# A macaron transformer kernel: the top-1 experts' bias-and-push product on four 32-row groups of TensorE, two tiles at a time, with three pairs of PSUM banks

## What is computed

```python
x = x + 0.5 * L0_ffn(layernorm(x))      # phase 0: F, 8 dense experts
x = x + L0_attn(layernorm(x))           # phase 1: R, RWKV mixing
x = x + 0.5 * L0_ffn(layernorm(x))      # phase 2: F
x = x + 0.5 * L1_ffn(layernorm(x))      # phase 3: E, top-1 of 8 experts
x = x + L1_attn(layernorm(x))           # phase 4: M, causal attention, 16 heads
x = x + 0.5 * L1_ffn(layernorm(x))      # phase 5: E

def L1_ffn(x):                          # D = 128, E = 8
    probs = softmax(einsum('bsd,ed->bse', x, router_w) + router_b)
    y_all = einsum('bsd,eod->bseo', x, expert_w) + expert_b
    return y_all[argmax(probs)] * max(probs)
```

## Time and profile before

| | us |
|---|---|
| median of 3 runs (1590.17 to 1595.67) | 1595.37 |
| profiled execution, whole | 1591.5 |
| its span in the trace | 1589.6 |
| PE busy in the span | 1541.5 (97%) |
| DVE busy in the span | 1260.2 (79%) |

### The profile page before, as it was taken

One profiled execution on the slowest core, in us unless ns is written; L12 is line 12 of the kernel. 1 busy time (PEld: TensorE's weight loads), 2 busy tenths in 40 slices (PEclk: granted clock), 3 DMA queues, 4 the chain that ended last, 5 costly groups with the idle time before them and its releaser, 6 DMA issues. The chain is left out here.

```text
span 1589.6 us, 43810 instructions
## 1 busy us (share of the span) xinstructions
PE 1541.5 (97%) x15808; PEld 922.1 (58%) x15808; DVE 1260.2 (79%) x2662; ACT 936.1 (59%) x1826; POOL 935.5 (59%) x806
## 2 busy tenths in 40 slices
PE   7999999999999899799999999999999999999999
PEld 4666666666666666566666666666654434444444
DVE  7976776777877788786777777768778899999877
ACT  6755555555656344365555555556553388888842
POOL 2865756757754399775766756657456334444453
PEclk9999999999999999999999999999999899999999
DMA  4300000000001242100000000000001121112011
GB/s 163 106 8 5 7 0 7 7 0 7 8 1 34 53 84 67 42 6 3 8 1 7 7 0 7 7 0 8 5 12 31 44 61 37 39 39 62 9 42 60
DMA packets 74315, 43.34 MB, mean 27 GB/s; under 512 B 53818, under 2 KB 70842, under 8 KB 74052
## 3 DMA queue, kind: packets, MB, share of 16 engines
q1 hardware_dynamic: 74180, 41.56, 10.9%
HBM read 10.47 MB, written 2.10 MB: 8 GB/s over the span
## 5 line engine op out<-in xcount | busy, mean ns | idle before, releaser
L618 POOL TENSOR_TENSOR scratch<-scratch 128x512 f16<-128x512 f32 x379 | 441.6, 1166 | 375.4 <-ACT scratch L826 375.2
L1395 DVE SCALAR_TENSOR_TENSOR scratch<-psum,scratch 128x512 f32<-128x512 f32 x512 | 352.4, 689 | 235.8 <-PE psum L1979 213.4
L821 ACT ACTIVATE scratch<-psum 128x512 f32<-128x512 f32 x512 | 305.2, 597 | 394.9 <-PE psum L1979 394.0
L2021 PE MATMUL psum<-ffn_down_hi,scratch 128*128 128x128 f16 x2048 | 369.3, 219 | 0.3
L2023 PE MATMUL psum<-ffn_down_hi,scratch 128*128 128x128 f16 x2048 | 369.2, 219 | 0.0
L2022 PE MATMUL psum<-ffn_down_lo,scratch 128*128 128x128 f16 x2048 | 369.2, 219 | 0.0
L826 ACT ACTIVATE scratch<-scratch 128x512 f16<-128x512 f32 x512 | 318.6, 622 | 12.0 <-DVE scratch L1395 11.7
L2021 PEld LDWEIGHTS psum<-ffn_down_hi,scratch 128*128 128x128 f16 x2048 | 200.3, 98 | 59.1 <-POOL scratch L618 0.7
L2022 PEld LDWEIGHTS psum<-ffn_down_lo,scratch 128*128 128x128 f16 x2048 | 200.4, 98 | 58.0
L2023 PEld LDWEIGHTS psum<-ffn_down_hi,scratch 128*128 128x128 f16 x2048 | 200.4, 98 | 0.0
L1977 PE MATMUL psum<-x_hi,ffn_gate_hi 128*128 (+1 forms) x512 | 194.5, 380 | 1.5 <-ACT scratch L821 1.5
(11 more groups left out here) (223 smaller groups left out, 2703.8 us busy)
## 6 DMA issues: line engine op xcount, KB each, us to landing
scratch<-scratch SPq DMA_DIRECT2D x96, 128.0 KB, 2.7
raw<-in_ffn_w_dram SPq DMA_DIRECT2D x8, 768.0 KB, 4.2
ffn_up_hi<-scratch SPq DMA_DIRECT2D x32, 128.0 KB, 2.8
x_tok<-in_x_dram SPq DMA_DIRECT2D x8, 256.0 KB, 7.2
out_dram<-x_tok SPq DMA_DIRECT2D x7, 256.0 KB, 2.2
raw<-in_lin_dram SPq DMA_DIRECT2D x1, 1092.0 KB
x_hi<-scratch SPq DMA_TRANSPOSE x46, 2.3
x_lo<-scratch SPq DMA_TRANSPOSE x46, 2.3
```

The source lines that it names most:

```text
L618: pool.tensor_tensor(h_lo[r], h32[r], h_hi[r], ALU.subtract).then_inc(s_plo, 1)
L821: act.activation(gate_act[k % 2], bank(k % 2), ACT.Silu, scale=W_DOWN).then_inc(s_s, 1)
L1395: dve.scalar_tensor_tensor(h32[k % HSLOTS], bank(5 + k % 2), W_DOWN, gate_act[k % 2], ALU.mult, ALU.mult).then_inc(s_h, 1)
L2021: pe.matmul(dst, h_hi[r][:, cols], hi, start=k % FC == 0 and n == 0, stop=False, skip_group_check=True)
```

## The change

The two matmuls of `bias_and_others` use only 10 rows of the array (8 pushes and 2 bias rows). Now their weights, and the rows that they meet, exist four times, on partitions 0, 32, 64 and 96. The bias's two halves of 512 columns stand beside each other on different partition groups (`e_bias`, loaded by 12 small DMAs from `bias_w` between the E phase's first and second `turn_x`). `e_not` has 128 columns for each tile (8 used in each of four groups of 32), so that `others` yields four copies of the rows. For two tiles together, four matmuls of 32 rows, each into a bank of its own, take the place of four with 128 rows. So in batches that have a next one, bias 0 moves behind products 1 and bias 2 behind products 3. In the last batch of a phase, and in the pieces woven into other phases, each tile's two matmuls are issued alone, also in 32-row form.

Tiles take the pairs of banks by `expert_banks`: three pairs in most of both phases, two at their borders. `products` waits for the pick of the last tile that had the same pair. `others` uses bank 6 in place of 4. `logits` adds the router's bias by one matmul of 32 columns for four tiles. PE's hardware loop over batches 2 to 5 is written out. A wait for the picks stands ahead of the attention's first projections.

```diff
-E_OUT = 2.0 ** 15
+E_OUT = 2.0 ** 14
+E_PUSH = 2.0 ** 16 - 2.0 ** 12
+E_GROUP = 32
...
-        e_not = carve(SUB * E, F16)
+        e_not = raw[:, 0:S // 2].bitcast(F16)
+        e_bias = raw[:, S // 2:S // 2 + BANK // 2].bitcast(F16)
...
+        def expert_banks(t):
+
+            if t < 2:
+                return t
+            if t < NS - 3:
+                return (2, 1, 0)[(t - 2) % 3]
+            if t < NS + SUB:
+                return t % 2
+            return (t - NS - SUB) % 3
+
+        def picked_before(t):
+
+            return 3 + max([s for s in range(t) if expert_banks(s) == expert_banks(t)], default=-1)
...
-            for b in range(3):
-                turn_x(3, b)
-            for b in range(3, NB):
+            turn_x(3, 0)
+            sp.wait_ge(s_erows, 3)
+            sp.wait_ge(s_blo, 2)
+            for i in range(4):
+                c = slice(i % 2 * BANK, (i % 2 + 1) * BANK)
+                row = i * E_GROUP
+                sp.dma_start(e_bias[row:row + E, :], bias_w[0:E, c]).then_inc(s_ebias, 16)
+                sp.dma_start(e_bias[row + E:row + E + 1, :], bias_w[32:33, c]).then_inc(s_ebias, 16)
+                sp.dma_start(e_bias[row + E + 1:row + E + 2, :], bias_w[64:65, c]).then_inc(s_ebias, 16)
+            for b in range(1, NB):
                 turn_x(3, b)
...
-                            for t in e_out:
-                                pool.memset(t, 1.0).then_inc(s_erows, 1)
+                            pool.memset(e_not, 1.0 / E_OUT).then_inc(s_erows, 1)
+                            pool.memset(e_bias, 0.0).then_inc(s_erows, 1)
...
-                    act.activation(e_out[odd][0:E, :], bank(at)[0:E], ACT.Copy, scale=E_OUT).then_inc(s_eout, 1)
+                    act.activation(e_out[odd], bank(at), ACT.Copy, scale=E_OUT).then_inc(s_eout, 1)
...
-                    dve.tensor_tensor(by(e_not, SUB), by(e_rank, SUB), over(e_first, SUB, E), ALU.not_equal).then_inc(s_enot, 1)
+                    rank = e_rank.rearrange("p (q o e) -> p q o e", q=SUB, o=1).to_broadcast([P, SUB, P // E_GROUP, E])
+                    first = e_first.rearrange("p (q o c) -> p q o c", q=SUB, o=1).to_broadcast([P, SUB, P // E_GROUP, E])
+                    dve.tensor_tensor(e_not.rearrange("p (q o c) -> p q o c", q=SUB, c=E_GROUP)[:, :, :, 0:E], rank, first, ALU.not_equal).then_inc(s_enot, 1)
...
-                    experts = psum[:, 2 * (k % 2) * BANK:2 * (k % 2 + 1) * BANK]
+                    at = 2 * expert_banks(t)
+                    experts = psum[:, at * BANK:(at + 2) * BANK]
...
+                    router_bias = bias_w[:, E * C:E * C + E].rearrange("p (o e) -> p o e", o=1).to_broadcast([P, SUB, E])
+                    pe.matmul(by(bank(7, 0, SUB * E), SUB), ones, router_bias, start=True, stop=True)
                     for q in range(SUB):
-                        dst = bank(7, q * E, (q + 1) * E)
-                        pe.matmul(dst, ones, bias_w[:, E * C:E * C + E], start=True, stop=False)
-                        ins = three(dst, parts(s + q), ecols(E * C, E * C + E), False)
+                        dst, (hi, lo), (w_hi, w_lo) = bank(7, q * E, (q + 1) * E), parts(s + q), ecols(E * C, E * C + E)
+                        pe.matmul(dst, hi, w_hi, start=False, stop=False, skip_group_check=True)
+                        pe.matmul(dst, hi, w_lo, start=False, stop=False, skip_group_check=True)
+                        ins = pe.matmul(dst, lo, w_hi, start=False, stop=True, skip_group_check=True)
...
-                def products(t, s, k, halves=range(2)):
-                    pe.wait_ge(s_epick, t + 1)
+                def products(t, s, halves=range(2)):
+                    pe.wait_ge(s_epick, picked_before(t))
                     for half_of in halves:
                         a = half_of * BANK
-                        three(bank(2 * (k % 2) + half_of), parts(s), ecols(a, a + BANK), True, False)
-
-                def bias_and_others(b, k, odd):
-                    if k == 0:
+                        three(bank(2 * expert_banks(t) + half_of), parts(s), ecols(a, a + BANK))
+
+                def bias_and_others(b, tiles, odd):
+                    if 0 in tiles:
                         pe.wait_ge(s_eout, b + 1)
-                    for half_of in range(2):
-                        a = half_of * BANK
-                        ins = pe.matmul(bank(2 * (k % 2) + half_of), e_out[odd][:, k * P:(k + 1) * P], bias_w[:, a:a + BANK], start=False, stop=True)
-                    ins.then_inc(s_ey, 1)
-
-                def others(b, at=4):
+                        if b == 0:
+                            pe.wait_ge(s_ebias, 12 * 16)
+                    for i, k in enumerate(tiles):
+                        for half_of in range(2):
+                            rows = slice((2 * i + half_of) * E_GROUP, (2 * i + half_of + 1) * E_GROUP)
+                            ins = pe.matmul(bank(2 * expert_banks(b * SUB + k) + half_of), e_out[odd][rows, k * P:(k + 1) * P], e_bias[rows, :],
+                                            start=False, stop=True, skip_group_check=True)
+                        ins.then_inc(s_ey, 1)
+
+                def others(b, at=6):
                     pe.wait_ge(s_enot, b + 1)
                     pe.wait_ge(s_eout, b)
+                    if b == NB + 2:
+                        pe.wait_ge(s_mout, NB)
                     for k in range(SUB):
-                        ins = pe.matmul(bank(at, k * P, (k + 1) * P)[0:E], e_not[:, k * E:(k + 1) * E], ident16, start=True, stop=True)
+                        ins = pe.matmul(bank(at, k * P, (k + 1) * P), e_not[:, k * P:(k + 1) * P], ident16, start=True, stop=True)
                     ins.then_inc(s_eoutp, 1)
...
-                            products(t0 + b * SUB + k, b * SUB + k, k)
-                            if use and isinstance(b, int) and b == 1 and k == 0:
+                            products(t0 + b * SUB + k, b * SUB + k)
+                            if use and b == 1 and k == 0:
                                 attention(plan[ph["i"] - 1], 3, False)
-                            if use and isinstance(b, int) and b == 1 and k == 1:
+                            if use and b == 1 and k == 1:
                                 attention(plan[ph["i"] - 1], 4, False)
-                            bias_and_others(b0 + b, k, odd)
+                            if not more:
+                                bias_and_others(b0 + b, (k,), odd)
+                            elif k % 2:
+                                bias_and_others(b0 + b, (k - 1, k), odd)
...
-                body(1, 1, False, True)
-                with pe.Fori(1, NB // 2 - 1) as pair:
-                    for odd in range(2):
-                        body(2 * pair + odd, odd, False, True)
-                body(NB - 2, 0, False, True)
+                for b in range(1, NB - 1):
+                    body(b, b % 2, False, True)
...
+                    pe.wait_ge(s_epick, NS - 3)
```

More of the change, by code:

```diff
@@ L328, in build @@
             "e_not_chosen_transposed", "e_not_chosen_rows")]
-        s_erows_in, s_erows = sem("e_rows_loaded"), sem("e_rows_set")
+        s_erows_in, s_erows, s_ebias = sem("e_rows_loaded"), sem("e_rows_set"), sem("e_bias_rows_placed")
         s_estep = sem("e_routing_step")
         E_STEPS = 4
+        def expert_banks(t):
[8 more added lines that the diff above has]
+            return 3 + max([s for s in range(t) if expert_banks(s) == expert_banks(t)], default=-1)
         s_ey, s_epick, s_ez, s_eadd = [sem(n) for n in ("e_experts_in_psum", "e_expert_picked", "e_weighted", "e_added")]
@@ L862, in late_weights @@
                         act.wait_ge(s_bhi, 2)
-                        act.activation(bias_w[0:E, 0:E * C], e_rows[0:E], ACT.Copy, scale=-E_OUT).then_inc(s_erows, 1)
+                        act.activation(bias_w[0:E, 0:E * C], e_rows[0:E], ACT.Copy, scale=-E_PUSH).then_inc(s_erows, 1)
                     if k == 5 and j == 0:
@@ L946, in weights, with others @@
                     act.activation(e_prob[odd], e_rec, ACT.Copy, scale=0.5 * W_DOWN).then_inc(s_eprob, 1)
-                def others(b, odd, at=4):
+                def others(b, odd, at=6):
                     act.wait_ge(s_eoutp, b + 1)
@@ L980, in moe @@
                     begin(act, ph["i"])
-                    others(b0, 0)
+                    others(b0, 0, 4)
                 def body(b, odd, prep, more):
@@ L1639, in moe @@
                 if use == 0 and start:
+                    dve.wait_ge(s_erows, 3)
                     route(b0)
@@ L2136, in moe @@
                     logits(b0, 0, n0 + LEAD)
-                    products(t0, 0, 0)
+                    products(t0, 0)
                 if use and start:
@@ L2147, in moe @@
                             pe.wait_ge(s_p1used, QT * UNITS + 1 + k)
-                        products(t0 + SUB * b + k, SUB * b + k, k, (what % 2,))
+                        products(t0 + SUB * b + k, SUB * b + k, (what % 2,))
```

(12 more changed lines are left out.)

## The result

| | before | after |
|---|---|---|
| median of 8 runs each, side by side, us | 1593.9 (1590.17 to 1596.99) | 1602.74 (1599.38 to 1608.53) |
| profiled execution; its span | 1591.5; 1589.6 | 1599.38; 1597.6 |
| PE busy; DVE busy | 1541.5; 1260.2 | 1531.3; 1263.1 |

The ratio is 1.0056, 95% interval [1.0042, 1.0069]: slower, by 8.8 us at the median. The interval leaves out 1, but it takes in 1.005, the smallest change that the prediction would call one. Forecast were 1594.5, no change, and a range that ends at 1602. Executions of one kernel scatter with the granted clock: of the changed kernel's eight the shortest, 1599.38, shows a mean of 0.993, the longest, 1608.53, one of 0.986. The traces explain the 7.9 us between the two profiled executions.

The account below looks back on a forecast made before the run. PE set the pace, DVE close behind; after the change a DVE-PE ring of 7.94 us a batch would. Phase 3 -0.2 and phase 5 +0.7 gave +0.5 us, 1592.0 profiled; forecast median 1594.5, range 1586 to 1602.

Parts of the forecast that it names:

- Four groups, 0.42 for two tiles: PE: four 32-row bias matmuls overlap, so two tiles cost 0.42 us instead of 0.86, bounds 0.22 and 1.06.
- Rival B: PE: the four row groups don't overlap, two tiles cost 1.06 us; +9.5 us, 1601 profiled, 1604; chance 0.08.
- select's last step: DVE: writes 128 elements instead of 32, 0.10 us more on 0.19, bounds 0 and 0.19.
- Phase 3, batch 0, +1.3: Pick 2 waits for bias 2 and 3, so pick 0 of batch 1 comes at 1195.9 instead of 1194.62.
- Batches 6 and 7, -0.8: End of phase 3: batch 6 bound by DVE at 7.36 us, batch 7 about 6.0; 13.4 instead of 14.2.
- The ring takes 7.94 us: Pick 0 to `e_not` on DVE, `others`, products 0, logits, products 1, bias product on PE, pick 0: 4.23 plus 3.71 us.
- Batches 1 to 5, -0.7: Phase 3: five batches at 7.94 us each instead of 40.40 us together.
- Phase 5, +3.1 and +1.2: Batches 0 and 1: DVE idles 3.1 us before batch 1's pick 0; late transfer puts batch 2's at +4.3.
- Batches 2 to 6, -3.6: Phase 5: three batches at 7.94 us, batch 5 at 7.04, batch 6 at 5.92; 36.8 instead of 40.36.
- The signs: Phase 3: picks 0 7.9 us apart, DVE waits some 0.6 ahead of each, PE over 1 ahead of `others`.
- Rival A: DVE alone bounds, batches 7.36 and 5.92 us; -9.5 us, 1582 profiled, 1585; chance 0.13.
- Rival C: TensorE's clock falls as PE idles 1.2 us a turn, in half of the turns: +14 us, 1608; chance 0.05.

Follow-up runs that it names:

- e13: Changed kernel with each tile's bias product issued alone and DVE's statistics ahead of the selection: ratio 0.9957 to the kernel before, median 1587.21 us.
- e12: Changed kernel with ScalarE's x_upper ahead of the weighing of tile 0 in all but two batches, one traced execution: 1598.12 us; timed earlier at ratio 1.0036.
- e2: Changed kernel with `others` moved behind products 0 of its own batch: ratio 1.0066 to the kernel before.
- e4: Kernel before with PE's hardware loop over batches 2 to 5 written out, nothing else: ratio 0.9974 to the kernel before.
- e7: Changed kernel without pairing, each tile's two 32-row bias matmuls directly behind its products: ratio 0.9966 to the kernel before.
- e11: Changed kernel, pairs kept, with logits behind the bias pair of tiles 0 and 1 and x_upper ahead of the weighing of tile 0: ratio 1.0004.
- e1: Changed kernel with the next batch's logits moved behind the bias product of tiles 0 and 1: ratio 0.9964 to the kernel before, median 1588.28 us.
- e6: Changed kernel with tiles 0 and 1 of phase 5's batch 1 unpaired: ratio 1.0021 to the kernel before.

## Why the prediction was wrong

Its sum was +0.5 on the profiled execution, and +7.9 came. By its own steps:

- *Four groups, 0.42 for two tiles:* right. The last full matmul starts at 1210.98; 0.215 later would be 1211.20, the four start at 1211.30, 0.10 behind that, and the next full matmul comes 0.32 later. Rival B is refuted. The Trainium skill, "TensorEngine Tiling (Array Packing)", Theoretical Speedup, gives up to four times for a dimension of at most 32. This trace agrees as far as it goes: four 32-row matmuls take the 0.32 that two of them take in e13. The drain at a change of mode, in Key Properties of the same page, has no price there; here a change costs 0.10. `others` 0.24 (0.22 forecast) and select's last step 0.29 (0.29) were right too.
- *Phase 3, batch 0, +1.3:* +1.33. *Batches 6 and 7, -0.8:* -0.6.
- **"The ring takes 7.94 us": the step that failed.** The selection's ring takes 7.96 (e12), but it is not the longest. `logits` stood in its sum as 0.33 of work, without what it waits for. The rows of before had the rest: pick 0 at 1202.35, the transpose at 1206.13, so 3.78 + 2.3 landing + 0.05 + 0.33 + 1.30 + 0.10 + 0.41 = 8.27, and 8.29 came. In the kernel before the same transfer had 1.9 us to spare.

Those two rows of before, and the logits that wait for the transfer:

```profile
1202.35 1.22 DVE L1627 TENSOR_REDUCE scratch<-psum 128x128 f32<-128x1024 f32 x1 [0.48 <-PE psum L2123]
...
1206.13 1.20 SPq L481 DMA_TRANSPOSE x_lo<-scratch  x1
...
1210.33 0.17 PE L2108 MATMUL psum<-scratch,half_sb 128*128 128x8 f16 x1
```

- *Batches 1 to 5, -0.7:* +3.4. Of the 4.1 between, 1.65 are the longer ring (0.25 in batch 1, 0.35 in each of the four others), and 2.45 are batch 4's own: 1.7 of late landing, and by the difference 0.75 for the clock.
- *Phase 5, +3.1 and +1.2:* +3.2 and +2.2. Here the prediction did follow the transfer, to the point: it was issued 7.47 behind pick 0 (7.43 forecast), and from logits to pick 0 it took 2.16 (2.19). The 0.9 more are a landing of 3.2 instead of 2.3.
- *Batches 2 to 6, -3.6:* -1.25. The x ring is most of this: three times 0.38, and 1.26 in batch 5, which took 8.30 instead of 7.04. Leaving out `prep_bn` shortens the selection's ring, but not the x ring. The transpose left 3.75 behind pick 0 as ever, and logits came 0.23 later than products 0 allowed (last matmul 1580.43):

```profile
1574.74 1.22 DVE L1654 TENSOR_REDUCE scratch<-psum 128x128 f32<-128x1024 f32 x1 [0.85 <-PE psum L2157]
...
1577.32 1.15 POOL L616 TENSOR_TENSOR scratch<-x_norm,scratch 128x512 f16<-128x512 f32 x1 [0.61 <-ACT scratch L829]
1577.34 1.18 DVE L1632 SCALAR_TENSOR_TENSOR scratch<-scratch,con_sb 128x32 f32<-128x32 f32 x1
...
1578.49 1.20 SPq L498 DMA_TRANSPOSE x_lo<-scratch  x1
...
1580.88 0.19 PE L2135 MATMUL psum<-scratch,half_sb 128*128 128x32 f16 x1
```

L1632, begun together with L616, took 1.18 there, which makes the selection's ring some 8.07. That is still shorter than the x ring, and in e2, with the selection's ring relieved, batch 5 took 8.29 all the same.

- *Together:* of the 7.4 us between forecast and result 4.0 are the x ring (1.65, 1.13 and 1.26), and 3.35 are the two late landings on it (2.45 and 0.9). Of the 1.26, 1.03 would have come through the stretched L1632 as well. The rest cancels.
- *Entry of phase 3 -0.7, phase 4 +0.5:* not in the sum. Over the traces of all runs the way from the last pick of phase 3 to the first of phase 5 took 269 to 277 us with its program unchanged. The 276 of e4 and e7 go with the clock: from 1250 to 1290 it was 0.60 and 0.63, or 0.62 and 0.61, in the two windows of 20 us, against 0.74 and 1.00 before. That is where single times scatter; the sums don't hold it.
- *The signs:* DVE idled ahead of pick 0 (0.84, forecast 0.6) and PE ahead of `others` (1.30, forecast over 1). Both came, though the ring that they were to show wasn't the one that ended last; e2 tells the two apart, these waits don't.
- *Rival A* is refuted for the change as made: DVE idles 0.84 ahead of each pick 0. Without pairing and with GpSimd's ring gone its 7.36 is 7.44 (e13). The Trainium skill's sentence in "TensorEngine Tiling (Array Packing)", PSUM Bottleneck, that the emptying of PSUM may then bound, agrees with e13 alone, not with the change as made.
- *Rival C:* the clock did fall, but behind the pauses that the transfer and the border made, not behind the turn's 1.3 us. In phase 5 it cost little, as PE waited again (1.07) ahead of logits.
- The spread: the range ended 0.7 below the result. It had no end for a landing later than the median, though the trace of before had one of 2.8 us in phase 3.

What stays open is why about one landing in a phase is late (3.2 and 4.0 us in the changed kernel), and why the clock stood lower in e11's longer executions. In phase 3 it is the same transfer, batch 4's, in after, e1, e2 and e6 (3.8 to 4.0), but in e7 and e12 it took 2.3.

## What to carry to other kernels

When two independent tiles are tied together by one group of instructions, list everything that is queued between them on that engine, and for each what it waits for: the new ring is the longest of those paths, and a transfer that had 2 us of slack is then on it, late landings and all. Close the ring for each such wait, from the rows of before, before trusting the shortest sum. A saving on the bounding engine is worth no more than the distance to the next engine, here 0.3 us a batch (7.73 in e4, 7.44 in e13); the pairing paid for it with 0.6 (8.29 against 7.73).

## What the runs showed of the hardware

- Four 32-row matmuls of 512 columns on four groups of rows, into four banks: 0.32 to the next full matmul, as two of them take, and 0.10 ahead for the change of form.
- A small DVE operation with both inputs in SBUF (128x32) took 0.56 us (e7) and up to 1.18 instead of 0.18 when a GpSimd operation of 128x512 with two inputs ran beside it: both ended together. Reductions from PSUM beside it kept their 1.22.
- The transposing DMA landed after 2.3 us in the median, and in the E phases after 2.8, 3.2, 3.8 or 4.0 at times. The one of 3.8 in e1 cost nothing, where logits start some 1.6 us behind the usual landing (1214.21 + 2.3 and 1218.08).
- The granted clock was at half (1.2 GHz) for some 3.4 us, once from 1 us after PE had resumed from a pause of 1.8 us, and once already when PE resumed from one of 3.4. With pauses of 1.3 us a turn it stayed at 1.00. Start to start, 512 columns took 0.43 us at half and 0.215 at full.
- A hardware loop on PE cost 0.44 us a batch (8.17 against 7.73 in e4).
